# Softmax maxima and subtractions of two head groups in one VectorE instruction over two PSUM banks

## What is computed

```
q = rope(x_ln @ Wq); k, v = split(ctx @ Wkv); k = rope(k)     # 32 heads of 8
w = softmax(q k^T / sqrt(8))          # over the 64 keys of the same sequence
x1 = x + (w v) @ Wout + bout
logits = l2norm(layernorm(x1)) . l2norm(mu)                   # 16 experts x 128 slots
slot_in = dispatch^T x_ln; h = gelu(slot_in W1 + b1); slot_out = h W2 + b2
out = x1 + combine slot_out
```

## Time and profile before

| | |
|---|---|
| median of 3 runs | 501.18 us (499.67 to 502.15) |
| the profiled execution | 498.91 us, its span 497.1 us |
| mean granted TensorE clock | 0.976 of full speed |
| TensorE busy, matmuls / weight loads | 446.1 / 382.3 us |
| VectorE, ScalarE, GpSimd busy | 351.5, 306.1, 146.0 us |
| maxima L704, subtractions L709 | 64 each, 41.0 and 40.9 us busy |
| attention exponentials L479 | 64, 38.9 us busy |
| the chain that ended last | TensorE 67%, VectorE 14%, issue 6%, ScalarE 3% |

### The profile page before, as it was taken

One profiled execution on the slowest core, in us unless ns is written; L12 is line 12 of the kernel. 1 busy time (PEld: TensorE's weight loads), 2 busy tenths in 40 slices (PEclk: granted clock), 3 DMA queues, 4 the chain that ended last, 5 costly groups with the idle time before them and its releaser, 6 DMA issues.

```text
span 497.1 us, 13916 instructions
## 1 busy us (share of the span) xinstructions
PE 446.1 (90%) x5296; PEld 382.3 (77%) x5296; DVE 351.5 (71%) x858; ACT 306.1 (62%) x611; POOL 146.0 (29%) x247
## 2 busy tenths in 40 slices
PE   0567799887999888999999999999999999999995
PEld 0446688876777767788888988888888888888884
DVE  5699598998899897665764764755755656666563
ACT  2347477776777767285476477467458458458544
POOL 2509611239969333014112112112112201211100
PEclk9959799999899899999999999999999999999999
DMA  6700000055003000000000000000000000000000
GB/s 163 271 7 7 7 7 7 9 146 128 7 5 73 0 2 1 1 2 12 12 2 13 12 0 11 11 0 11 11 0 11 11 0 11 11 11 0 12 13 12
DMA packets 16016, 12.72 MB, mean 26 GB/s; under 512 B 7232, under 2 KB 15344, under 8 KB 15600
## 3 DMA queue, kind: packets, MB, share of 16 engines
q1 hardware_dynamic: 15984, 12.27, 8.7%
HBM read 10.16 MB, written 2.11 MB: 25 GB/s over the span
## 4 chain that ended last, share of the span: by engine, by line
PE 67%; DVE 14%; issue 6%; POOL 3%; ACT 3%; DMA 3%; SPq 2%; DVEq 0%; POOLq 0%; ACTq 0%
PE psum L959 14%; PE psum L961 13%; PE psum L960 13%; PE psum L1164 9%; PE psum L1179 6%; DVE mx L704 4%; PE psum L1005 3%; PE psum L1020 2%; PE psum L1053 2%; DVE pb L709 2%; PE psum L1037 2%; DVE pb L873 2%; ACT mu_raw L568 2%; DVE kT L699 1%; DMA ctile<-in_ctx 1%
## 5 line engine op out<-in xcount | busy, mean ns | idle before, releaser
L568 ACT COPY mu_raw<-psum 128x384 f32<-128x384 f32 x96 | 41.0, 445 | 104.5 <-PE psum L1164 104.5
L851 DVE TENSOR_REDUCE es<-eb 128x4 f32<-128x512 f32 x64 | 43.1, 686 | 63.1 <-ACT eb L560 63.1
L1164 PE MATMUL psum<-w_raw,eb 64*128 64x129 f32 x1024 | 66.6, 279 | 1.1 <-DVE pb L873 0.2
L1164 PEld LDWEIGHTS psum<-w_raw,eb 64*128 64x128 f32 x1024 | 60.5, 187 | 6.4 <-DVE pb L873 4.2
L350 POOL TENSOR_TENSOR sm<-sm,mhalf 128x1 f32<-128x1 f32 x16 | 8.8, 551 | 166.4 <-DVE sm L830 166.4
L959 PE MATMUL psum<-mun_h,xlT_l 128*128 128x512 f32 x128 | 52.6, 411 | 0.2 <-DVE xlT_l L837 0.2
L873 DVE TENSOR_TENSOR pb<-psum,rh 128x384 f32<-128x384 f32 x96 | 49.3, 513 | 3.3
L960 PE MATMUL psum<-mun_l,xlT_h 128*128 128x512 f32 x128 | 50.7, 396 | 0.0
L961 PE MATMUL psum<-mun_h,xlT_h 128*128 128x512 f32 x128 | 50.7, 396 | 0.0
L479 ACT ACTIVATE pb<-pb 128x512 f32<-128x512 f32 x64 | 38.9, 633 | 14.1 <-DVE pb L709 14.1
L483 ACT COPY pT<-psum 128x512 f32<-128x512 f32 x64 | 34.7, 592 | 19.0 <-PE psum L1020 18.8
(11 more groups left out here) (156 smaller groups left out, 1049.2 us busy)
## 6 DMA issues: line engine op xcount, KB each, us to landing
mu_raw<-in_L_ffn_mu SPq DMA_DIRECT2D x1, 2048.0 KB, 13.2
out<-w_raw SPq DMA_DIRECT2D x16, 128.0 KB, 1.7
xa<-in_x SPq DMA_DIRECT2D x1, 1536.0 KB, 9.2
ctile<-in_ctx SPq DMA_DIRECT2D x16, 64.0 KB, 2.4
eb<-mur_scratch SPq DMA_DIRECT2D x1, 1024.0 KB, 5.0
w_raw<-in_L_ffn_W SPq DMA_DIRECT2D x2, 512.0 KB, 8.0
w_raw<-in_L_ffn_W SPq DMA_DIRECT2D x1, 1024.0 KB, 9.1
xa<-in_x SPq DMA_DIRECT2D x1, 512.0 KB, 3.4
```

Source lines behind the costliest of these rows:

```text
L568: a.copy(eT[:, e0:e0 + n, :].rearrange("p n (b k) -> p b n k", b=2), pair(i, n)[:, :, :, HC:XC]).then_inc(eT_ready, 1)
L851: v.reduce_sum(es[:, 4 * c:4 * c + 4], eb[:, 4 * c:4 * c + 4, :], AX.X).then_inc(es_ready, 1)
L1164: m = mm(bank[HB[i % 3] + b][:, n * XC:(n + 1) * XC], eb[rows, e, :], xw[rows, e, :], start=True, stop=True)
```

## The change

One maximum and one subtraction are issued for two groups at once, over banks g0 and g0+1 (1024 elements in a row instead of 512). The maximum waits until both groups are filled; each subtraction raises `sub_done` once for two groups, so ScalarE's two exponentials of a pair wait for the same value. The exponentials themselves stay apart, one a group. TensorE's waits on `sub_done` count to 2 a step instead of 4.

```diff
             def exp_group(t, p, gr):
-                act.wait_ge(sub_done, t * 4 + gr + 1)
+                act.wait_ge(sub_done, t * 2 + gr // 2 + 1)
                 a.activation(pb[:, p, gr], pb[:, p, gr], ACT.Exp, scale=HD ** -0.5).then_inc(p_ready, 1)
...
-            def softmax_max(t, gr):
-                dve.wait_ge(s_filled, t * 4 + gr + 1)
-                v.reduce_max(mx[:, gr, :], bank[gr][:].rearrange("p (h k) -> p h k", k=SEQ), AX.X)\
-                    .then_inc(max_done, 1)
-
-            def softmax_sub(t, p, gr):
-                dve.wait_ge(max_done, t * 4 + gr + 1)
-                v.tensor_tensor(pb[:, p, gr], bank[gr][:].rearrange("p (h k) -> p h k", k=SEQ),
-                                mx[:, gr, :].unsqueeze(2).broadcast_to([P, 8, SEQ]), ALU.subtract)\
-                    .then_inc(sub_done, 1)
-
             def softmax(t, p, g0):
-                for gr in (g0, g0 + 1):
-                    softmax_max(t, gr)
-                for gr in (g0, g0 + 1):
-                    softmax_sub(t, p, gr)
+                src = psum[:, g0:g0 + 2, :].rearrange("p g (h k) -> p (g h) k", k=SEQ)
+                top = mx[:, g0:g0 + 2, :].rearrange("p g h -> p (g h)")
+                dve.wait_ge(s_filled, t * 4 + g0 + 2)
+                v.reduce_max(top, src, AX.X).then_inc(max_done, 1)
+                dve.wait_ge(max_done, t * 2 + g0 // 2 + 1)
+                v.tensor_tensor(pb[:, p, g0:g0 + 2].rearrange("p g h k -> p (g h) k"), src,
+                                top.unsqueeze(2).broadcast_to([P, 16, SEQ]), ALU.subtract).then_inc(sub_done, 1)
...
-                wait(pe, sub_done, t * 4)
+                wait(pe, sub_done, t * 2)
...
-            pe.wait_ge(sub_done, TILES * 4)
+            pe.wait_ge(sub_done, TILES * 2)
```

## The result

The changed kernel took 504.48 us in the median of 7 runs (503.6 to 508.86), against 501.18 in the median of 7 (499.67 to 502.15). The medians are 3.3 us apart. The ratio estimated over all these runs is 1.0082, 95% interval 1.0051 to 1.0114: slower by some 4 us (2.6 to 5.7). Its profiled execution took 503.88 us with a span of 502.1, 5.0 more than before.

A forecast was written before the change was run, and what follows sets the result against it. It took the attention stage's chain of waits, with both softmax calls of a step on it, as the bound. Terms 2.5 + 0.4 + 1.0 + 0.1 - 0.6 = +3.4 us gave 504.6 us on the median, range 501.4 to 507.4.

The forecast's parts named there:

- VectorE gains 0.05 a call: Each softmax call on VectorE, up to the end of the last subtraction, falls from 2.48 to 2.43 us.
- The -0.6 of the sum: VectorE's saving of 0.05 us on 12 calls on the path: nine second-call halves and three calls before step 2.
- the fixed part really goes: Rival on VectorE: a call saves 0.34 us instead of 0.05, time 499.7 us, not slower; chance 0.15.
- stall: Rival on VectorE: joint instructions stall, a call takes up to 2.71 us, time 507.0 us; chance 0.12.
- 5 us of busy time: VectorE sheds 64 x (1.28 - 1.20) = 5 us of busy time while the kernel still gets slower.
- The oT copy 0.52 late: First call on ScalarE: second exponential starts 0.52 us later, delaying oT; +0.50 net in steps 9, 11, 12, 14, 15, +2.5.
- Steps 4 to 6, 0.34 each by the copy of v: Second call on ScalarE: late copy of v delays TensorE's transposes by 0.34 us, three times, +1.0 us.
- Steps 7 and 8 at nothing: Two delays of 0.5 us fit under TensorE's later 2.00 us wait for a context tile: 0; without this cover +1.0.
- Steps 10 and 13, 0.2 each: First matmuls at half clock, exponentials already late: oT 0 to 0.4 us later each, 0.2 taken, +0.4 for both.
- Everything behind step 15 is a TensorE queue that starts this much later: nothing there is added or hidden.: After the last attention step, TensorE's work moves by the sum of +3.4 us, with nothing added or hidden.
- More half-clock stretches: Rival on TensorE: new idle pieces bring further half-clock logits at 0.9 us each, three of them 507.3 us; chance 0.10.
- other steps than 10 and 13: Sign of being wrong: steps other than these two run cold, that is at half clock on TensorE.

The follow-up runs named there:

- first_call_joint: Only the first softmax call of a step (groups 0 and 1) joint, the second as in the kernel before; ratio to the kernel before 1.0077.
- joint_oT_between: The changed kernel with ScalarE's oT copy between the exponentials of groups 0 and 1 instead of behind both; ratio to the kernel before 0.9980.
- joint_oT_between_v_first: The changed kernel with oT copied between the first two exponentials and v copied ahead of those of groups 2 and 3; ratio to the kernel before 1.0004.
- joint_again: The changed kernel once more, unaltered; ratio to the kernel before 1.0072.
- joint_k_wait_last: The changed kernel with TensorE's wait for the subtractions put ahead of its wait for kT, now last before the logits; ratio to the kernel before 1.0067.
- split_oT_between_v_first: The kernel before, with oT copied between the first two exponentials and v copied ahead of those of groups 2 and 3; ratio to the kernel before 0.9997.
- second_call_joint: Only the second softmax call of a step (groups 2 and 3) joint, the first as in the kernel before; ratio to the kernel before 0.9982.

## Why the prediction was right, and where it was not

The forecast was 504.6, the median 504.48, and the mechanism is the one stated: the late second exponential, not VectorE. That the numbers agree to 0.1 is luck. The forecast was 3.4 above a median of 501.18; in the later comparisons the kernel before had 500.2 to 500.3, and the difference was 4. Term by term:

- **VectorE gains 0.05 a call.** Mis-sized: 0.01. The instructions took 1.215 and 1.224, not 1.20; the gap of 0.03 was right. The -0.6 of the sum was about -0.1. The rival "the fixed part really goes" wanted 2.14 a call and has 2.47; the "stall" one wanted up to 2.71. VectorE did not shed 5 us of busy time: 3.8 in the two groups, 0.4 in all. The figure of the Trainium skill ("VectorE: DVE Perf Modes", "Side-by-side: where the cycles go for N=2048 bf16") is right as a length: 1024 plus 158 cycles at 0.96 GHz are 1.23 us, measured 1.22. It did not give the saving, because here most of the fixed part was already hidden under a neighbour (starts 0.60 apart, 0.68 long).
- **The oT copy 0.52 late.** Right: 0.56 with the 0.04 up to the subtractions, twice 0.5 by experiment (first_call_joint puts it there, joint_oT_between takes it away). A late step grew by 0.68 and 0.59, not by 0.45, because of VectorE's smaller gain and 0.13 between kT and the logits in every other step, which I had not seen coming. (The 0.63 of one exponential is not in rows 10; the page of the kernel before has 633 ns as the mean of L479.)
- **Steps 4 to 6, 0.34 each by the copy of v.** Right in kind (joint_oT_between_v_first takes it out), and 0.40 and 0.41 in size, again without the -0.05.
- **Steps 7 and 8 at nothing.** Right: step 7 grew by 0.70, step 8 lasted 11.37 before and 10.58 changed, so the two together took 0.09 less. The wait for the context tile took the delay.
- **Steps 10 and 13, 0.2 each.** Step 10 grew by 0.38, with its logits at half clock again (2.02 us, before 1.83). Step 13 kept its full clock this time and took 10.68 instead of 11.18. Together -0.1 instead of +0.4.
- **"Everything behind step 15 is a TensorE queue that starts this much later: nothing there is added or hidden."** Wrong for this execution: 2.3 us of half clock at the end.
- **Not in the sum at all: the clock ahead of step 4.** TensorE's wait ahead of the transposes of step 2 was 2.55 us before and ended at 53.20; its clock then fell. In the changed kernel's profile the clock fell earlier, from about 43 to 50 us; step 2 came later, the wait was gone, and the clock stayed up. The windows from 54 to 56 us, first of the kernel before, then of the changed one (granted clock third from last):

```profile
54.00:56.00 2.00, 2.00 (x42) 2.00 (x42) 0.10 (x1) 1.38 (x3) 1.81 (x4) 0.50 0.11 33
```

```profile
54.00:56.00 2.00, 2.00 (x64) 1.83 (x61) 1.97 (x3) 1.78 (x6) 1.81 (x4) 1.00 0.12 33
```

The 1.35 us by which step 4 starts earlier are this execution's and not shown to be the change's. In `joint_again`, the same kernel, step 4 starts at 70.22, after the kernel before. In the timeline of `joint_k_wait_last`, with both calls joint, the wait is there again, and its clock falls behind it as before:

```profile
54.09 0.44 PE L963 MATMUL psum<-ident,xn 128*128 128x128 f32 x2 [2.24 <-POOL xn L367]
```

And `split_oT_between_v_first`, without any joint instruction, goes without this wait (its step 2 takes 11.55 us; before 14.05, changed 11.70). Over all profiles the logits of step 4 start between 67.48 and 71.74.

So the sum of 3.4 came near the measured 4 partly by luck. The steps in which the sum has one of the two delays decide at full clock (4 to 6, 9, 11, 12, 14 and 15) took 4.2 us more, where it has 3.2 for them. Steps 7, 8, 10 and 13 took 0.2 less, where it has 0.3 more, and outside these steps the span of this profile moved by -1.35 ahead of step 4 and by +2.3 at the end. "More half-clock stretches" was listed as a rival for late steps; it was not seen. From step 4 on, one group of logits ran at half clock in the changed kernel (step 10) and one in `joint_again` (step 8, 1.91 us; "other steps than 10 and 13" was named as a sign of being wrong), against two before.

## What to carry to other kernels

Joining two instructions on one engine also joins their two signals. Look at what is queued behind the consumers: here a copy that had nothing to do with the softmax stood behind two exponentials and paid one exponential a step. Moving it between the two took that half microsecond out of the steps again. And price an instruction by the time from its start to the next one's: where neighbours overlap as here, most of the fixed part is hidden already, and a join that makes two dependent instructions adjacent gives the overlap up. Before crediting or blaming a change of under 1%, compare the step times and the granted clocks, not the totals alone.

## What the runs showed that was not expected

The mean granted clock differs between kernels that do the same matmuls, and the time hangs on it in part. The kernels with four instructions a call, before among them, had 0.967 to 0.970 over their timed executions, joint_oT_between 0.979. Over 30 executions of the kernel before, in one of the three comparisons, the clock ran from 0.959 to 0.979 and the time from 498.0 to 505.8 us; in the three, 0.01 less clock goes with 1.3 to 2.4 us more (correlation -0.4 to -0.6).

The profiles show where such time lies. Steps 4 to 14 took 115.22 us before and 114.39 in joint_oT_between, whose late steps are longer (10.16 and 10.07 against 9.99 and 10.00): before had steps 10 and 13 partly at half clock, 2.3 us above its other late steps together, and joint_oT_between had none. With both calls joint, the six profiles have 0, 0, 1, 1, 1 and 2 groups of logits above 1.5 us from step 4 on; seven of the eight other profiles have 2, one has 1.

What sets this is open. The guess in the expectations was that idle time in smaller pieces keeps the clock up. The traces speak against it: at full clock a late step of second_call_joint (10.16 us, mean clock 0.977) has TensorE idle for 1.2 us with pieces up to 0.76, and one of split_oT_between_v_first (9.63 us, 0.967) for 1.0 us with pieces up to 0.53. No run changed the idle pieces alone.
